# Transpositions that nobody reads in four more gaps at the beginning of an attention and feed-forward kernel, and the fourth pair's maximum scores ahead of the fifth pair's queries and keys

## The reference

```python
x = x + attention(layernorm(x), Wq, Wk, Wv, Wp, bp)      # 16 heads of 64
x = x + ffn(layernorm(x), ln1_g, ln1_b, w1, b1, ln2_g, ln2_b, w2, b2)   # 128 -> 512 -> 128

# attention, per batch and head
q = (x @ Wq[h]) / 8 ;  k = x @ Wk[h] ;  v = x @ Wv[h]
out = softmax(q @ k.T) @ v            # heads interleaved feature by feature, then @ Wp + bp
# ffn: layernorm, times ternary(w1) + b1, exact gelu, layernorm, times ternary(w2) + b2
```

## Time and profile before

| | us |
|---|---|
| median of 3 runs | 1022.97 |
| lowest, highest | 1022.38, 1025.62 |
| span of the profiled execution | 1023.9 |

### The profile page before, as it was taken

How to read it: one execution, slowest core, us unless ns; L and a number is a source line. 1 busy time by engine, 2 the same in 40 slices (tenths; PEclk the granted TensorE clock), 3 DMA queues, 4 the chain that set the end, 5 groups by cost and what they waited for, 6 DMA issues and landing times.

```text
span 1023.9 us, 39195 instructions
## 1 busy us (share of the span) xinstructions
PE 994.6 (97%) x16031; PEld 785.4 (77%) x16031; DVE 867.6 (85%) x1756; ACT 717.6 (70%) x1091; POOL 881.6 (86%) x860
## 2 busy tenths in 40 slices
PE   7989999999999999999999999999999999889998
PEld 5667777877777877777777778777778777678886
DVE  6898888888788888888888888888888888468998
ACT  5677666767666667666766766676667677768995
POOL 5789999998899999999999999999999997847675
PEclk8999999999999999999999999999999999989999
DMA  6112323132433232223322332233233232333332
GB/s 139 36 29 52 51 51 64 34 50 51 72 50 50 41 64 50 52 51 72 52 51 46 55 68 42 41 51 71 51 52 51 52 51 46 65 63 66 81 79 68
DMA packets 203665, 57.82 MB, mean 56 GB/s; under 512 B 185056, under 2 KB 203232, under 8 KB 203488
## 3 DMA queue, kind: packets, MB, share of 16 engines
q1 hardware_dynamic: 201408, 54.79, 29.7%
q10 hardware_dynamic: 2080, 0.52, 0.2%
HBM read 7.21 MB, written 4.19 MB: 11 GB/s over the span
## 4 chain that ended last, share of the span: by engine, by line
PE 89%; DVE 5%; DMA 2%; ACT 2%; issue 2%; POOL 0%; SPq 0%; DVEq 0%; POOLq 0%; ACTq 0%
PE S L586 15%; PE PV L608 8%; PE S L578 7%; PE PV L610 6%; PE PV L609 6%; PE QK L543 5%; PE QK L545 5%; PE QK L544 5%; PE M L556 5%; PE misc L642 3%; PE misc L644 3%; PE misc L643 3%; PE S L731 2%; PE misc L622 2%; PE misc L624 2%; PE misc L623 2%
## 5 line engine op out<-in xcount | busy, mean ns | idle before, releaser
L1023 POOL TENSOR_TENSOR pl<-p 128x1024 f16<-128x1024 f32 x256 | 485.4, 1896 | 66.4 <-ACT p L837 65.7
L837 ACT ACTIVATE p<-S,s_exp 128x1024 f32<-128x1024 f32 x256 | 285.4, 1115 | 123.1 <-PE S L586 122.9
L1200 DVE TENSOR_REDUCE negmax<-M 128x4 f32<-128x1024 f32 x252 | 307.5, 1220 | 49.5 <-PE M L556 46.2
L845 ACT ACTIVATE QKh<-QK 128x512 f16<-128x512 f32 x251 | 149.8, 597 | 135.1 <-PE QK L545 135.0
L608 PEld LDWEIGHTS PV<-V,p 128*128 128x128 bf16 x2048 | 185.7, 98 | 63.4 <-issue 39.2
L608 PE MATMUL PV<-V,p 128*128 128x65 f16 x2048 | 216.7, 194 | 8.8 <-DVE O L1214 6.8
L1220 DVE TENSOR_TENSOR QKl<-QK,QKh 128x512 f16<-128x512 f32 x251 | 172.9, 689 | 52.5 <-ACT QKh L845 51.8
L609 PE MATMUL PV<-V,p 128*128 128x64 f16 x2048 | 214.4, 193 | 0.0
L610 PE MATMUL PV<-V,pl 128*128 128x65 f16 x2048 | 213.6, 194 | 0.0
L609 PEld LDWEIGHTS PV<-V,p 128*128 128x128 bf16 x2048 | 189.8, 98 | 0.0
L610 PEld LDWEIGHTS PV<-V,pl 128*128 128x128 f16 x2048 | 189.4, 97 | 0.0
(11 more groups left out here) (188 smaller groups left out, 2253.2 us busy)
## 6 DMA issues: line engine op xcount, KB each, us to landing
result<-X SPq DMA_DIRECT2D x16, 256.0 KB, 2.5
X<-in_L_attn_query SPq DMA_DIRECT2D x7, 512.0 KB, 5.7
OT<-O SPq DMA_TRANSPOSE x64, 4.4
shift<-negmax SPq DMA_TRANSPOSE x63, 2.3
O<-in_L_attn_Wk ACTq DMA_DIRECT2D x2, 256.0 KB, 4.4
O<-in_L_attn_Wq SPq DMA_DIRECT2D x2, 256.0 KB, 4.8
O<-in_L_attn_Wv SPq DMA_DIRECT2D x1, 512.0 KB, 4.3
w<-in_L_ffn_w SPq DMA_DIRECT2D x2, 256.0 KB, 6.4
```

Source lines behind the costliest of these rows:

```text
L837: e.activation(p32[r][:, :, :, :].rearrange("p i m n -> p (i m n)"), S[:, :], ACT.Exp, scale=s_exp[:, :]).then_inc(s_ex, 1)
L1023: e.tensor_tensor(pl[r][:, :, :, :].rearrange("p i m n -> p (i m n)"), p32[r][:, :, :, :].rearrange("p i m n -> p (i m n)"), p_high(r).rea ...
L1200: e.tensor_reduce(dst[:, :, NB * jj:NB * jj + NB], max_bank(p)[:, :].rearrange("p (i t m) -> p i t m", i=2, t=NB), AX.X, ALU.max, negate=T ...
```

## The change

Four groups of unread transpositions are added to TensorE's list: 6 ahead of the maximum scores of pair 0 (into S), 6 ahead of the spreading of the values' maximum (into M, after the first maximum), 3 ahead of the maximum scores of pair 3 (into S, after the second maximum), and 6 ahead of the transposition of the first shift (into its own bank). `kept_busy` gets the bank as an argument. The maximum scores of pair 3 are issued before the queries and keys of pair 4, and the transposition of the first shift before the maximum scores of pair 4. The lists of the other engines stay as they are.

```diff
             def first_shift_turned():
                 dst = misc_take("shift", 0)
+                kept_busy(6, dst)
                 e.wait_ge(s_mx, GP)
                 e.transpose(dst[:, 0:P], first_max[:, :, :].rearrange("p i c -> p (i c)"), ident[:, :]).then_inc(s_sht, 1)
...
-            def kept_busy(n):
+            def kept_busy(n, bank=S):
 
                 for _ in range(n):
-                    e.transpose(S[:, 0:P], ident[:, :], ident[:, :])
+                    e.transpose(bank[:, 0:P], ident[:, :], ident[:, :])
...
             queries_keys(0)
+            kept_busy(6)
             max_scores(0)
             queries_keys(1)
             maxima_turned("v", "part_v")
             queries_keys(2)
             max_scores(1)
+            e.wait_ge(s_mx, 1)
+            kept_busy(6, M)
             maxima_spread("v")
             queries_keys(3)
             max_scores(2)
+            e.wait_ge(s_mx, 2)
+            kept_busy(3)
+            max_scores(3)
             queries_keys(4)
-            max_scores(3)
+            first_shift_turned()
             max_scores(4)
-            first_shift_turned()
```

## The result

The changed kernel takes 1021.18 us in the median of 22 runs (1019.34 to 1023.3), the kernel before 1023.08 in 22 runs beside it (1020.84 to 1026.43). The ratio is 0.9978, with a 95% interval of 0.997 to 0.9986: 0.22% faster, 1.4 to 3.1 us, 1.9 by the medians. Forecast were 1022.0 and a gain of 1.0 us. The way is as forecast and the time inside the range, but the gain is about twice as large, and more than the mechanism that was worked out can give.

The account below looks back on a forecast made before the run. TensorE was taken to bound the span, still waiting for others in the first 30 us. Gains of 0.58 us (order, earlier shift) and 0.4 (clock) made 1.0 off 1022.97, so 1022.0 at chance 0.60; range 1020.0 to 1024.6.

Parts of the forecast that it names:

- The fillers cost nothing: The added transpositions fit TensorE's idle gaps in the beginning; the first two groups cost nothing, 0.1 us at most each.
- parts 1 to 4: The four transposition groups of 6, 6, 3 and 6, the last two with the moves in order; six take 0.82 us.
- The mechanism of the beginning: First 30 us: sixth pair's maximum scores at 26.1 instead of 27.06, 1.0 us off, bounds 0.1 to 1.1.
- the fourth maximum: VectorE's reduction for the fourth pair starts at 19.75 instead of 20.83 us, right behind the third.
- the first exponential: On ScalarE, at 24.42 us instead of 25.00, with no ScalarE idle time since the first shift's rounding.
- the sixth pair's maximum scores: On TensorE, at 26.1 us instead of 27.06, released by ScalarE's high part.
- the rounding's 0.38 us of wait on ScalarE: First shift's rounding, begun at 22.69 us, could start once ScalarE is free at 22.31: 0.38 us to be had.
- the order and the earlier shift: Beginning: 0.58 us of the gain, 0.38 from the rounding plus 0.2 from the fifth pair's earlier high part.
- Part 4's hole on VectorE: VectorE idles 0.6 us before the fifth maximum because the first shift's transposition goes ahead of that pair's maximum scores.
- The clock: TensorE keeps 2.4 GHz from 19.5 to 26.5 us; two pairs' queries and keys off half clock give 0.4 us.
- C: End of attention, 880 to 920 us: one further low-clock stretch costs 1.7 us, 0.7 slower, 1023.7; chance 0.10.
- D: End of attention, 880 to 920 us: one of two low-clock stretches is gone, 1.7 + 1.0 us, 1020.3; chance 0.10.

Follow-up runs that it names:

- Order only: Changed kernel without its 21 added transpositions, keeping the two moves in TensorE's order; 1023.75 us, ratio 0.9996 against the kernel before.
- transpositions only: Changed kernel with its four groups of transpositions but the old order of TensorE's work; 1020.59 us, ratio 0.9973 against the kernel before.
- the run without the last move: Changed kernel with the first shift transposed behind the fifth pair's maximum scores again; 1021.35 us, ratio 0.9977 against the kernel before.
- a longer list: Kernel before with 40 more TensorE instructions: 11 unread small products replace 2 of 24 unread transpositions at the very beginning; 1022.69 us, ratio 0.9995.
- moved weights on the kernel before: Kernel before with two preparations of feed-forward weights on ScalarE two steps later; 1023.51 us, ratio 0.9999.

## Why the prediction was right, and where it wasn't

**The fillers cost nothing: right.** Cover and price were as worked out for parts 1 to 4: six take 0.82 us from first start to last end, and each instruction behind a group starts where its own data lets it.

**The mechanism of the beginning: right in size, wrong in its parts.** 1.0 us forecast, 1.11 measured between two profiles. The steps came within 0.3 us, counted from each profile's first reduction: the fourth maximum at 5.30 us (forecast 19.75 - 14.44 = 5.31), the first exponential at 9.87 (forecast 9.98), the sixth pair's maximum scores at 11.51, released by ScalarE (forecast 11.66). But the sum gave 0.58 us to the order and 0.4 to the clock. Order only gives 0.2 to 0.3 us in the profile and no time that can be measured; transpositions only give all but 0.07 us. The step that failed is the one that gives the rounding's 0.38 us of wait on ScalarE to "the order and the earlier shift". They go away at the upper clock in the old order too (0.07 us are what is left), because that wait was itself made of matmuls at half clock. In order only they go as well, but the clock falls 0.24 us earlier there (5.02 us behind the first maximum and not 5.26), the fifth pair's high part comes 0.23 us later for it, and the rounding gains 0.24 us in all. A step that two parts of a change can each take away was booked to one of them.

**Part 4's hole on VectorE: right and empty.** 0.78 us instead of the 0.6 forecast, without effect, as the run without the last move shows.

**The clock: right that it holds.** In eight of eight profiles with the change's transpositions it holds to the end of the beginning. Of the six without, it falls in four and holds in two (one of these with other products in place of two of the 24 transpositions). So the low clock of the earlier trace rows was not a fixed cost of the kernel before, and the 1.1 us are what a run saves in which it would have fallen. The forecast read one execution as if it were all.

**The size of the whole: wrong by half.** Missing terms in the sum: waits for the shift's transposition near 206 and 220 us (0.4 to 1.0 us less in the profiles of the changed list), and the one near 880 us (1.5 to 1.6 us, in every profile whose list has the length of before up to there and in none with a longer one; among profiles with equally many low stretches at the end, the last of the three stretches in the table is 0.9 to 1.9 us shorter without it). Both were in the trace: the second is the 1.6 us of TensorE's waits shown above, and it ends at 880.4 us, 0.4 us inside the first of the two windows that I had read for the low clock. I took that stretch as something that could only be struck by luck of the clock. This wait in it is struck by the length of TensorE's list. Rivals C and D named the right place with a cause that is only a part: the profile after does have one low stretch there and not two, as D said, but the wait is gone beside it. At 1.7 us a stretch they were priced too high. One stretch, 3.4 us at half, costs 1.1 to 1.3 us, as the first three groups of the 22 runs of the change show, which lie one such stretch apart: mean span 1017.8 us at a mean clock of 1.000 (2 runs), 1019.0 at 0.998 (10), 1020.1 at 0.997 (6), 1020.9 at 0.996 (4).

**The range.** Its upper end doesn't follow from its own words: C's 1023.7 with half of the upward scatter of 2.65 us gives 1025.0 and not 1024.6. And the far halves of C and D, at 0.10 each, leave 1 in 10 outside, not 1.5. That 1021.18 fell inside is in part luck: the 0.8 us by which it lies under the forecast come from terms that the sum didn't have.

**What stays open.** The pieces of the profiles, 1.1, 0.8 and 1.5 us, add up to 3.4, more than the 1.9 measured (1.4 to 3.1). That the first is not in every run explains a part. At a mean clock of 1.000 only the two later pieces, 2.3 us by these profiles, can be left, and 1.5 us are. Neither of them is shown by the median of a kernel that has it alone: a longer list gave 0.5 us with 1.0 either way, moved weights on the kernel before 0.1 with 0.95 either way where the profile has 0.7 to 0.9. Open are why a longer list had more runs at a low mean clock, and how an instruction packet holds up the last packets of a transposition. What is shown by time: the transpositions carry the whole gain, the order by itself none that can be measured, and the gain stays at 2.1 us when the end of attention is filled in both. That more of it comes from the length of the list than from the clock is what the runs by their mean clock say, together with the moved wait; a kernel with the change's list length and with no low clock in any run wasn't run.

## What to carry to other kernels

A profile is one execution: compare its time with the median before a difference of two profiles is taken off that median, and look at a second profile before a low clock is booked as a fixed cost. Where each run's mean clock is on record, compare runs at the same one: medians can hide a gain that is there in every line. When a change lengthens an engine's list, look for transfers that a wait depends on and for instruction packets beside them, and follow two traces by a marker that occurs at every step; the gain may lie 200 or 800 us behind the edit. Unread work in a gap costs nothing while the instruction behind it is held by another engine, and filling the two longest gaps of the kernel (2.3 us each) was worth two thirds of the change itself (0.15% against 0.22%).

## What the runs showed of the hardware

- The same DMA transposition of 128 by 128 fp16 took from 2.2 to 4.5 us to land. It took 2.2 to 2.5 us in all 549 cases with no instruction packet on its way between 1 us behind the issue and the landing. In the fifteen cases near 202 and 216 us with a 16 KB instruction packet beside it, it landed 1.0 to 1.2 us after that packet's end. Near 876 us it took 2.7 to 3.0 us in nine profiles and 4.1 to 4.3 in the five in which a 16 KB packet started about 1 us behind its issue. Such a packet takes 0.9 to 1.7 us itself.
- From 16 to 20 us TensorE was busy 2.30 of 4.00 us both in the kernel before and in the one with weights moved, with the same list up to there: the clock fell to 1.2 GHz at 19.70 us in the one and stayed at 2.4 GHz in the other. Of the four executions with this list it fell in three.
- Around the two idle times of 2.3 us ahead of the last weighted sums, the clock was at half in one or two stretches in all ten profiles that leave them unfilled; with 18 transpositions in each it was in none, in four of four.
